# Softmax sums by four products behind the next unit's first scores, and unit one's queries ahead

## The reference

```
def _L0_attn_ref(x, W_DQ, W_UQ, W_QR, W_DKV, W_UK, W_UV, W_KR, W_O):
    ...
    q = jnp.concatenate([q_C, q_R], axis=-1)
    k = jnp.concatenate([k_C, k_R], axis=-1)
    scores = jnp.einsum('bhqd,bhkd->bhqk', q, k)
    scores = jnp.clip(scores, -80.0, 80.0)
    scores = jnp.where(causal[None, None], scores, -jnp.inf)
    weights = jax.nn.softmax(scores / jnp.sqrt(jnp.float32(d_qk)), axis=-1)
    attn = jnp.einsum('bhqk,bhkd->bhqd', weights, v)
    ...
x = x + _L0_attn_ref(xn, ...) + _L0_ffn_ref(xn, ...)
```

## Time and profile before

| | us |
|---|---|
| median of 3 runs | 1305.17 |
| lowest, highest | 1304.73, 1306.3 |
| profiled execution | 1304.52 |
| its span in the trace | 1302.7 |
| PE busy in it | 1280.0 |
| GpSimd, VectorE, ScalarE busy | 628.1, 723.2, 648.4 |

### The profile page before, as it was taken

One profiled execution on the slowest core, in us unless ns is written; L12 is line 12 of the kernel. 1 busy time (PEld: TensorE's weight loads), 2 busy tenths in 40 slices (PEclk: granted clock), 3 DMA queues, 4 the chain that ended last, 5 costly groups with the idle time before them and its releaser, 6 DMA issues.

```text
span 1302.7 us, 20569 instructions
## 1 busy us (share of the span) xinstructions
PE 1280.0 (98%) x6251; PEld 1048.3 (80%) x6251; DVE 723.2 (56%) x1349; ACT 648.4 (50%) x1163; POOL 628.1 (48%) x535
## 2 busy tenths in 40 slices
PE   5999999999999999999999999999999999999998
PEld 4788898888888888888887688887888888887886
DVE  6472255322222222222224787888888888888787
ACT  6411133222222222222225677777777777777775
POOL 5124567995060003200001577677766777676543
PEclk9999999999999999999999999999999999999999
DMA  8236654664151213312113143333243323322012
GB/s 297 68 107 236 218 200 142 181 193 142 58 162 50 66 55 104 109 58 66 50 50 102 59 99 65 63 50 63 41 80 50 54 51 65 63 44 61 18 50 98
DMA packets 82167, 123.34 MB, mean 95 GB/s; under 512 B 20176, under 2 KB 28496, under 8 KB 82064
## 3 DMA queue, kind: packets, MB, share of 16 engines
q1 hardware_dynamic: 48912, 56.43, 15.5%
q0 software_dynamic: 11312, 27.23, 9.7%
q10 hardware_dynamic: 21840, 38.36, 9.2%
HBM read 74.41 MB, written 39.05 MB: 87 GB/s over the span
## 4 chain that ended last, share of the span: by engine, by line
PE 90%; POOL 3%; DVE 2%; issue 1%; DMA 1%; ACT 1%; SPq 1%; ACTq 0%; POOLq 0%; DVEq 0%
PE bank L49 84%; PE bank L1513 2%; PE bank L1454 2%; PE bank L1596 1%; DMA rot_sin<-sum_b 1%; DMA staging<-in_wsg 1%; POOL rot_sin L583 0%; POOL sum_b L614 0%; POOL sum_b L611 0%; POOL rot L588 0%; POOL sum_b L616 0%; SPq L435 0%; ACT rows_b L651 0%; DVE store_b L1350 0%; DVE acc L1377 0%
## 5 line engine op out<-in xcount | busy, mean ns | idle before, releaser
L49 PE MATMUL bank<-store_b,store_a 128*128 128x512 f32 (+1 forms) x1536 | 318.7, 359 | 3.2 <-issue 1.2
L49 PE MATMUL bank<-slots,x_turned 128*128 x1296 | 317.5, 394 | 0.3 <-DVE x_turned L973 0.3
L49 PEld LDWEIGHTS bank<-store_b,store_a 128*128 128x128 f32 x1536 | 256.2, 189 | 59.9 <-issue 9.0
L49 PEld LDWEIGHTS bank<-slots,x_turned 128*128 128x128 f32 x1296 | 239.2, 188 | 48.2 <-issue 0.7
L995 DVE TENSOR_TENSOR hid_t<-bank,hid_t 128x512 fp32r<-128x512 f32 x70 | 48.4, 691 | 339.3 <-ACT hid_t L682 339.3
L49 PE MATMUL bank<-slots,hid_t 128*128 (+1 forms) x840 | 208.5, 397 | 0.0
L49 PE MATMUL bank<-store_b 128*128 128x512 f32 x768 | 180.3, 390 | 1.2 <-ACT bank L886 1.0
L49 PEld LDWEIGHTS bank<-slots,hid_t 128*128 128x128 f32 x840 | 153.6, 188 | 31.5 <-DVE hid_t L995 0.8
L49 PEld LDWEIGHTS bank<-store_b 128*128 128x128 f32 x768 | 143.8, 188 | 32.3 <-issue 2.2
L1350 DVE TENSOR_TENSOR store_b<-p_store,store_b 128x512 fp32r<-128x512 f32 x128 | 137.5, 1076 | 25.8 <-ACT store_b L867 25.7
L676 ACT ACTIVATE hidden<-bank 128x512 f32<-128x512 f32 x70 | 41.8, 598 | 205.0 <-PE bank L49 205.0
(11 more groups left out here) (202 smaller groups left out, 1773.0 us busy)
## 6 DMA issues: line engine op xcount, KB each, us to landing
staging<-in_w SPq DMA_DIRECT2D x56, 256.0 KB, 2.7
sorted_y<-y_store ACTq DMA_DIRECT2D x54, 256.0 KB, 2.0
rows<-sorted_x ACTq DMA_DIRECT2D x51, 260.0 KB, 2.7
rot_sin<-sum_b SPq DMA_DIRECT2D x128, 64.0 KB, 2.0
staging<-in_wg SPq DMA_DIRECT2D x28, 256.0 KB, 2.8
y_store<-in_x ACTq DMA_DIRECT2D x16, 256.0 KB, 3.4
shared_y<-y_store ACTq DMA_DIRECT2D x16, 256.0 KB, 2.3
raw<-in_wot SPq DMA_DIRECT2D x16, 256.0 KB, 2.8
```

The lines of the kernel that those rows point to most:

```text
L49: made = pe.matmul(out, a, b, start=first and n == 0, stop=last and n == len(pairs) - 1, skip_group_check=onto)
```

## The change

- `sums` has four products. GpSimd adds the first half of group 2 into the second half of group 0 in `p_store`, in place, once group 0's low part is made; ScalarE rounds the sum into the new tile `sum_a_hi`, GpSimd subtracts into `sum_a_lo`, and these two are multiplied by `unit_r` where the parts of groups 0 and 2 were.
- On PE the sums of unit u - 1 stand behind the first scores of unit u. Rounding and subtracting for a unit wait for `o_done` of the unit before where they waited for `dens_done`.
- On ScalarE `sums_row` of the unit before comes first in a unit, ahead of the exponents; `rotate_high` comes ahead of the rounding of `sum_b`. On SyncE the divisors of the unit before go out ahead of the halves' swap.
- On GpSimd the rotation stands ahead of the additions to `sum_b`.
- For unit one, the rotary product, its swap and the two queries come one feed-forward block sooner, or ahead of the second part of the head weights; the two transfers of the rotary tables come behind the swap.

```diff
@@ -243,6 +243,8 @@
         rot_raw = sum_b[:].rearrange("p h t -> p (h t)")
+        sum_a_hi = tile(ctx, "sum_a_hi", [P, BANK], F32R, side="right")
+        sum_a_lo = tile(ctx, "sum_a_lo", [P, BANK], F32R, side="right")
         sems(*(f"x_in{n}" for n in range(NT)), "scattered0", "scattered1", "padded0", "padded1", *(f"staged{n}" for n in range(NS)), *(f"row_in{n}" for n in range(3)),
...
@@ -303,13 +305,15 @@
+        ring.take("query", 0, 0)
+        ring.take("query", 0, 1)
...
-        ring.take("query", 0, 0)
...
-        ring.take("query", 0, 1)
...
+                if g == 0 and u:
+                    ring.take("sums", u - 1)
...
@@ -318,13 +322,10 @@
                     ring.take("output", u - 1, tt)
-            if u:
-                ring.take("sums", u)
             for h in heads_of(u):
...
                 ring.take("head", p + 1, h, 1)
-            if not u:
-                ring.take("sums", u)
+        ring.take("sums", NU - 1)
         for tt in range(TB):
...
@@ -356,9 +357,9 @@
             v, f = divmod(n, NG)
-            dve.wait_ge(on["sum_step"], 3 * v + 3)
+            dve.wait_ge(on["sum_step"], 4 * v + 4)
             if f == 0:
-                dve.wait_ge(on["p_low0"], v + 1)
+                dve.wait_ge(on["first_low"], v + 1)
             else:
...
@@ -435,20 +436,31 @@
                     sp.dma_start(rot_sin[b:c, :], rot_raw[a:b, :]).then_inc(on[f"rot_swapped{u % 2}"], 16)
+            def send_divisors(u):
+                sp.wait_ge(on["rows_made"], u + 1)
+                if u >= 2:
+                    sp.wait_ge(on["ratio_made"], u - 1)
+                for s in range(2):
+                    sp.dma_start(sum_store[:, u % 2, s].rearrange("p h t -> p (h t)"),
+                                 divisor_rows[s:s + 1, :].rearrange("o (p c) -> o p c", p=P)).then_inc(
+                        on[f"divisor_sent{u % 2}"], 16)
+
             rotary_weights(0)
...
             head_weights(0, 1)
+            swap_halves(0)
             sp.wait_ge(on["turned"], NBK)
...
             sp.dma_start(sin_t[:], rope_sin_t).then_inc(on["rope_in"], 16)
-            swap_halves(0)
             for h in range(2):
...
             for u, (p, b) in enumerate(units):
+                if u:
+                    send_divisors(u - 1)
                 if u + 1 < NU:
...
@@ -461,13 +473,7 @@
                     head_weights(p + 1, h)
-                sp.wait_ge(on["rows_made"], u + 1)
-                if u >= 2:
-                    sp.wait_ge(on["ratio_made"], u - 1)
-                for s in range(2):
-                    sp.dma_start(sum_store[:, u % 2, s].rearrange("p h t -> p (h t)"),
-                                 divisor_rows[s:s + 1, :].rearrange("o (p c) -> o p c", p=P)).then_inc(
-                        on[f"divisor_sent{u % 2}"], 16)
+            send_divisors(NU - 1)
             for tt in range(TB):
...
@@ -600,23 +606,31 @@
                 if u:
-                    pool.wait_ge(on["dens_done"], u)
+                    pool.wait_ge(on["o_done"], 2 * u)
                 pool.tensor_tensor(p_lo[0], prob(u, 0), p_hi[0].bitcast(F32), ALU.subtract).then_inc(on["p_low0"], 1)
                 w = [prob(u, g).rearrange("p (h t) -> p h t", h=2) for g in range(NG)]
+                w1_q1 = prob(u, 2)[:, 0:2 * P].rearrange("p (h t) -> p h t", h=2)
                 w3_q3 = prob(u, 2)[:, 2 * P:4 * P].rearrange("p (h t) -> p h t", h=2)
+                pool.wait_ge(on["p_low0"], u + 1)
+                pool.wait_ge(on["exps_done"], NG * u + 3)
+                pool.tensor_tensor(w[0][:, :, P:2 * P], w[0][:, :, P:2 * P], w1_q1, ALU.add).then_inc(
+                    on["sum_step"], 1)
                 if u + 1 < NU:
                     sine(u + 1)
+                pool.wait_ge(on["first_high"], u + 1)
+                pool.tensor_tensor(sum_a_lo[:], prob(u, 0), sum_a_hi[:].bitcast(F32), ALU.subtract).then_inc(
+                    on["first_low"], 1)
+                if u + 1 < NU:
+                    rotate(u + 1)
                 pool.wait_ge(on["exps_done"], NG * u + 4)
...
                 pool.wait_ge(on["exps_done"], NG * u + 5)
-                pool.wait_ge(on["sum_step"], 3 * u + 1)
+                pool.wait_ge(on["sum_step"], 4 * u + 2)
                 pool.tensor_tensor(sum_b[:], sum_b[:], w[4], ALU.add).then_inc(on["sum_step"], 1)
-                pool.wait_ge(on["sum_step"], 3 * u + 2)
+                pool.wait_ge(on["sum_step"], 4 * u + 3)
                 pool.tensor_tensor(sum_b[:, :, P:2 * P], sum_b[:, :, P:2 * P], w3_q3, ALU.add).then_inc(
                     on["sum_step"], 1)
-                if u + 1 < NU:
-                    rotate(u + 1)
                 pool.wait_ge(on["sums_high"], u + 1)
...
@@ -812,7 +826,9 @@
                     silu(b)
-                if b == NBK - 1:
+                if b == NBK - 2:
+                    act.wait_ge(on["turned"], NBK - 1)
+                    act.wait_ge(on["scale_made"], NR - 1)
                     rotate(0)
...
@@ -890,15 +906,17 @@
             head_weights(0, 1, 0)
+            rotate_high(0)
             evict(NBK - 2)
+            query(0, 0)
+            hid_high(NBK - 1)
+            query(0, 1)
             head_weights(0, 0, 1)
-            hid_high(NBK - 1)
-            rotate_high(0)
-            query(0, 0)
             head_weights(0, 1, 1)
-            query(0, 1)
             evict(NBK - 1)
             for u, (p, b) in enumerate(units):
+                if u:
+                    sums_row(u - 1)
                 exponents(u, 0)
...
@@ -907,6 +925,8 @@
                 exponents(u, 3)
+                act.wait_ge(on["sum_step"], 4 * u + 1)
+                act.activation(sum_a_hi[:], prob(u, 0), ACT.Copy).then_inc(on["first_high"], 1)
                 exponents(u, 4)
...
@@ -920,10 +940,10 @@
                     query(u + 1, 1)
-                act.wait_ge(on["sum_step"], 3 * u + 3)
-                act.activation(sum_b_hi, sum_b[:], ACT.Copy).then_inc(on["sums_high"], 1)
                 if u + 1 < NU:
                     rotate_high(u + 1)
+                act.wait_ge(on["sum_step"], 4 * u + 4)
+                act.activation(sum_b_hi, sum_b[:], ACT.Copy).then_inc(on["sums_high"], 1)
                 if b == 1 and p + 1 < PAIRS:
...
@@ -934,8 +954,6 @@
                                    ACT.Copy).then_inc(on["o_high"], 1)
-                if u < NU - 1:
-                    sums_row(u)
                 for h in heads_of(u):
...
@@ -1386,12 +1404,12 @@
                                   ALU.mult).then_inc(on["ratio_made"], 1)
+            rotate_low(0)
+            query(0, 0)
+            hid_low(NBK - 1)
+            query(0, 1)
             head_weights(0, 0, 1)
-            hid_low(NBK - 1)
-            query(0, 0)
-            rotate_low(0)
             head_weights(0, 1, 1)
-            query(0, 1)
             for u, (p, b) in enumerate(units):
...
@@ -1647,8 +1665,9 @@
                     turn_block(1)
+                if b == NBK - 2:
+                    rotate(0)
                 if b == NBK - 1:
-                    rotate(0)
                     head_weights(0, 0, 0)
...
@@ -1717,10 +1736,8 @@
                 row = ring.bank("sums", u)[0:2, :]
-                second_half = row.rearrange("p (h t) -> p h t", h=2)[:, :, P:2 * P]
-                product(pe, row, [(unit_r[:, 0, :], s[0]) for s in (p_hi, p_lo)], last=False)
-                product(pe, second_half, [(unit_r[:, 0, :], s[2][:, 0:2 * P].rearrange("p (h t) -> p h t", h=2))
-                                          for s in (p_hi, p_lo)], first=False, last=False)
+                pe.wait_ge(on["first_low"], u + 1)
+                product(pe, row, [(unit_r[:, 0, :], sum_a_hi[:]), (unit_r[:, 0, :], sum_a_lo[:])], last=False)
                 pe.wait_ge(on["sums_low"], u + 1)
...
@@ -1749,17 +1766,18 @@
                     made.then_inc(on["o_done"], 1)
-                if u < NU - 1:
-                    sums(u)
-
+
+            query(0, 0)
+            turn_hidden(NBK - 1)
+            query(0, 1)
             head_weights(0, 0, 1)
-            turn_hidden(NBK - 1)
-            query(0, 0)
             head_weights(0, 1, 1)
-            query(0, 1)
             down(NBK - 1)
             for u, (p, b) in enumerate(units):
-                scores(u, (0, 1))
+                scores(u, (0,))
+                if u:
+                    sums(u - 1)
+                scores(u, (1,))
                 if u + 1 < NU:
```

10 lines of the change are left out of this document (5 added, 5 removed).

## The result

| | before | after |
|---|---|---|
| median of 4 runs, us | 1304.95 | 1370.82 |
| lowest, highest | 1304.49, 1306.3 | 1367.32, 1372.61 |
| profiled execution, span | 1304.52, 1302.7 | 1372.51, 1370.6 |

The ratio is 1.0501, with a 95% interval of 1.0488 to 1.0515: the changed kernel is 66 us slower. Forecast were 1365 us and a range of 1330 to 1395. The profiled execution is 1.7 us above the median.

The account below looks back on a forecast made before the run. PE's own stream bounded the kernel; next would be the VectorE-GpSimd round of turns. Terms 35.7 + 15.6 + 3.1 + 2.5 - 1.2 + 4 = 59.7 on 1304.5 gave 1364, 1365 us on the median's scale; range 1330 to 1395.

Parts of the forecast that it names:

- Both waits that the prediction named for PE: PE idle before the next unit's first scores (query subtraction) and before their fourth product (second rotary half).
- The second hole: PE's wait before the fourth product of the next scores, until 20.66 us, for VectorE's second rotary half.
- the ledger: Timed steps of a steady unit, zero at its first scores: 19.98 us per unit instead of 17.89.
- Part one: PE's sums: four products instead of six, 0.93 us instead of 1.16, 7.4 us less over 32 units.
- Part two: Added per unit: GpSimd addition (0.68 us taken) and subtraction (1.15 to 1.29 us), ScalarE copy (0.63 us).
- Part three, the turns: Moved work in a steady unit: VectorE and GpSimd turns delay queries and rotary halves, 2.1 us without head weights.
- The rival on the rotary halves: 64-partition rotary halves take no turns with GpSimd: step 18.9 us, 1334 us in all; chance 0.17.
- The faster rival: VectorE's group 4 goes ahead of GpSimd's first sum, so PE never waits: 1296 us; chance 0.08.
- The sum: All terms over the whole kernel: 59.7 us added to 1304.5, giving 1364 us.
- The mis-sized term: SyncE's queue: long divisor DMAs in 7 of 32 units move the halves, 4 us in all.
- The start: Unit one's rotary part and queries sooner: the 1.23 us PE hole goes, 1.2 us back.
- Row copy ahead of the exponents: On ScalarE the sum row's copy comes first, so the rotary copy ends at 5.23 us instead of 4.35.

Follow-up runs that it names:

- Experiment 12: Four products, both low parts of the sums on VectorE, ScalarE, VectorE and GpSimd work reordered, against a 1317.99 us version with the same PE order: 1296.61 us.
- experiment 9: The changed kernel with GpSimd's first addition to sum_b waiting for VectorE's subtraction of group 4: 1352.12 us.
- experiment 1: The kernel before with only unit one's rotary part and queries sooner: 1302.9 us, ratio 0.9985.
- Experiment 4: The kernel before with only the sums, row copy and divisors moved, plus ScalarE's rotary copy ahead of group 1's exponents: 1321.87 us, against 1328.12 without that.

## Why the prediction was right

The bound, the direction and the cause came out as forecast. By its steps, with the profiled executions:

- **What bounds after.** PE's stream became shorter and stopped being the bound; the round of turns between VectorE and GpSimd took its place. Both waits that the prediction named for PE are the two largest in the table, and of the waits in attention the sums stand third with 3.8 us. The second hole is as forecast: from the first to the fourth product 2.35 us, by the ledger 20.66 - 18.33 = 2.33. The first is longer, 1.13 us where the ledger had 0.67.
- **Part one** held: 0.92 us for four products against 0.93 forecast. Experiment 12 shows the saving by itself. From the first scores to the end, it takes 1294.0 - 704.7 = 589.3 us and the kernel before 1302.7 - 706.3 = 596.4: 7.1 us, 7.4 forecast.
- **Part two.** The added subtraction took 1.30 us beside nothing and up to 1.75 behind a turn. The added addition of 256 columns took 0.74 us (0.68 taken), between its bounds; GpSimd's other addition of 256 columns takes 0.73 us in after (L632, the median of 32 units), so the 1.28 us of L616 held some 0.5 us of a turn.
- **Part three, the turns.** With zero at the fourth product less 0.68 us, 1055.42, and the rotary copy of that unit (L769) at 1060.21 to 1060.79, the trace gives (forecast in brackets): rotary copy ends 5.37 (5.23), sine starts 10.12 (9.23), queries end 18.96 (18.3), L635 ends 20.83 (20.08), second half ends 21.38 (20.63). All that follows is 0.6 to 0.9 us late, nearly all of it since the sine started 4.75 us behind the rotary copy instead of 4.00. Where it starts 4.0 to 4.1 us behind, ten of twelve steps are 20.2 to 20.3 us, against 19.98 forecast.
- **The rival on the rotary halves** is out. An operation on 64 partitions takes its turn like one on 128: L1277 took 1.69 us at 1075.11, right behind L1276's 0.69. The Trainium skill, "SBUF — State Buffer", section "Who interferes with whom", calls the shared port pair an exclusive lock and says that the order of issue, not the shape of the operation, decides who waits. The trace agrees: L635 was issued 0.54 us ahead of L1277, and 0.69 became 1.69 us.
- **The faster rival** is out as it was stated: its turn alone is worth 19 us (experiment 9), not 75. Its time, 1296 us, is that of PE's shorter stream without holes. Experiment 12 reaches it (1296.61) by another way, with the turns away from both results, the queries and the half; that is no point for the rival.
- **The sum.** From the first scores to the end after takes 1370.6 - 709.0 = 661.6 us, 65.2 more than before; forecast for this stretch were 60.9. The first two steps cost 4.1 us (22.71 and 20.20 against 20.64 and 18.21) where 3.1 were given. The 28 steady steps cost 58.9 (573.3 - 514.4), where 29 had been given 51.3, and 4 for long divisor transfers. The forecast counted one steady step without head weights too many, 17 for 16. (Steps are differences of the starts of successive sums; the last one, 12.9 us after and 14.0 before, has no unit behind it and is counted with the tail.) The split was off: with head weights 1.5 us per step (1.3 forecast), without 2.6 (2.1, the upper end of the 1.7 to 2.6 given), so that both kinds last 20.4 to 20.5 us: the head weights hide wholly in the hole. What is left, 2.2 us, is the first sums and the tail (2.5 forecast); the last sums wait 1.80 us for L635. Over the whole span the loss is 67.9 us; the other 2.6 stand ahead of the first scores, where the wait at 208 us and the low clock behind it took more than the start gave.
- **The mis-sized term** is SyncE's queue. All pairs of divisor issues took 1.12 to 1.21 us, none of the long ones of the earlier trace rows came again. The four issues of the halves' swap took their place: from the start of the first to the end of the fourth they last 2.46 us nearly always in before, and 2.41 to 3.20 in after, with single ones of 1.02 us as the row of L436 shows. Worked out from the timelines of the units from the third on (the rotary part of the very first, with 6.97 us in after, is made in the feed-forward part), the sine starts 4.36 us behind the rotary copy on the mean, 4.09 before: 0.27 us for 30 steps is 8 us at most, where 4 were given. That the delay makes the steps longer is read from the trace; no run takes it away. Why issues on that queue are longer at that time was not tried.
- **The start** gained 1.7 us (experiment 1), 1.2 forecast. In the profile of after this gain is covered by the wait at 208 us.
- **Row copy ahead of the exponents** was given as the reason for the late rotary copy. Experiment 4 shows that reason in part only: exponents of group 1 stood in front as well, and behind both the sums in PE's own stream.

## What to carry to other kernels

An operation on an engine at half load can hold up a bound engine, if it shares a turn with the work which that engine waits for: here two operations of 1.30 and 0.74 us on GpSimd cost 36 us, 1.2 us per unit. Count turns per round and ask in front of which result they pile up; moving the last one away only shows the one before. In this kernel the saving on the bound engine was taken in full only when the helpers' turns had been placed as well: the same four products gave 66 us of loss in one order, and 8 us of gain in another that also has both low parts on VectorE.
